# The last stage of a four-stage transformer kernel: chunks of 512 tokens, a wider window for its scatters, and results of a token side by side

## What is computed

```
xn = (x1 - mean(x1)) * rsqrt(var(x1) + 1e-5) * ln_gamma + ln_beta
abel_out = gelu(xn @ abel_w + abel_b)
logits = xn @ moe_gate_w + moe_gate_b            # 8 experts
topw, topi = top_k(logits, 2);  topw = softmax(topw)
h  = gelu(xn @ ew1[e] + eb1[e])                  # 128 -> 256, for the two experts of a token
eo = h @ ew2[e] + eb2[e]                         # 256 -> 128
moe_out = sum of the two eo, weighted by topw
moe_out = moe_out @ expm(gens[0]) @ expm(gens[1]) @ expm(gens[2])
gate = sigmoid(concat(abel_out, moe_out) @ gc_w + gc_b)     # one number per token
result = x + x1 + abel_out * (1 - gate) + moe_out * gate
```

## Time and profile before

| | us |
|---|---|
| time, median of 3 runs (1953.77 to 1956.29) | 1954.69 |
| the profiled execution, its own time | 1961.08 |
| its span, first to last instruction | 1959.3 |
| PE busy over the span | 1404.7 |
| DVE busy | 1144.8 |
| ACT busy | 684.6 |
| POOL busy | 658.8 |

### The profile page before, as it was taken

One profiled execution on the slowest core, in us unless ns is written; L12 is line 12 of the kernel. 1 busy time (PEld: TensorE's weight loads), 2 busy tenths in 40 slices (PEclk: granted clock), 3 DMA queues, 4 the chain that ended last, 5 costly groups with the idle time before them and its releaser, 6 DMA issues.

```text
span 1959.3 us, 36114 instructions
## 1 busy us (share of the span) xinstructions
PE 1404.7 (72%) x13280; PEld 931.6 (48%) x13280; DVE 1144.8 (58%) x3564; ACT 684.6 (35%) x1106; POOL 658.8 (34%) x903
## 2 busy tenths in 40 slices
PE   4587878788887888786347994777777956737750
PEld 2344434343434444343335663666666846636640
DVE  4576667768686767663543552666766653224437
ACT  1144444444444444444102341232333311124532
POOL 2022232323132222221141003566666725534442
PEclk9599999999999999998558996677767655557885
DMA  3646355452727253540611110111111120112224
GB/s 94 99 70 94 49 76 87 70 93 32 121 34 117 37 89 62 89 71 10 220 31 37 37 37 19 49 49 35 36 35 32 30 75 32 40 59 64 67 60 114
DMA packets 88673, 125.06 MB, mean 64 GB/s; under 512 B 17376, under 2 KB 62949, under 8 KB 87604
## 3 DMA queue, kind: packets, MB, share of 16 engines
q1 hardware_dynamic: 80004, 108.90, 29.2%
q0 software_dynamic: 7392, 13.39, 2.2%
q10 hardware_dynamic: 1104, 0.48, 0.1%
HBM read 30.15 MB, written 19.34 MB: 25 GB/s over the span
## 4 chain that ended last, share of the span: by engine, by line
PE 37%; DVE 28%; issue 8%; DMA 8%; POOL 8%; ACT 5%; SPq 4%; DVEq 0%; ACTq 0%; POOLq 0%
PE S L392 5%; DVE first L588 5%; PE A L421 4%; PE S L871 4%; SPq L330 3%; PE S L384 3%; PE S L403 3%; DMA yq<-yq,id 3%; DVE S L593 3%; POOL xq L1874 2%; DVE sc L1373 2%; DVE mx L1372 2%; DMA Kp<-rck 2%; PE A L1229 2%; PE S L166 2%
## 5 line engine op out<-in xcount | busy, mean ns | idle before, releaser
L495 ACT ACTIVATE P<-S 128x1024 f32<-128x1024 f32 (+3 forms) x384 | 310.1, 809 | 402.2 <-PE S L403 398.7
L662 POOL TENSOR_SCALAR_AFFINE_SELECT P<-P 128x256 f32<-128x256 f32 (+1 forms) x256 | 114.8, 450 | 546.1 <-ACT P L495 546.0
L392 PE MATMUL S<-Kp,Qp 120*128 120x512 f32 (+3 forms) x768 | 240.9, 399 | 77.1 <-DMA Kp<-rck 48.3
L403 PE MATMUL S<-Qp,Kp 121*128 121x512 f32 (+3 forms) x768 | 238.2, 394 | 71.7 <-DVE first L588 25.8
L593 DVE CUSTOM_DVE_ANT_0 S<-S,later 128x512 f32<-128x512 f32 (+3 forms) x512 | 239.8, 515 | 64.8 <-PE S L392 64.0
L392 PEld LDWEIGHTS S<-Kp,Qp 120*128 120x128 f32 x768 | 130.6, 201 | 217.3 <-issue 89.7
L588 DVE TENSOR_REDUCE first<-S 128x2 f32<-128x1024 f32 x128 | 156.6, 1224 | 117.0 <-PE S L392 116.5
L403 PEld LDWEIGHTS S<-Qp,Kp 121*128 121x128 f32 x768 | 133.8, 198 | 151.1 <-DVE first L588 46.0
L421 PE MATMUL A<-P,V 128*9 128x512 f32 (+3 forms) x1536 | 180.0, 516 | 3.7 <-POOL P L662 3.7
L1304 ACT ACTIVATE pr<-sc 128x1024 f32<-128x1024 f32 x32 | 34.3, 1072 | 208.6 <-DVE sc L1373 208.6
L1879 POOL DMA_INDIRECT yq<-yq,id x71 | 72.7, 1024 | 89.7 <-DVE yq L1825 74.6
(11 more groups left out here) (311 smaller groups left out, 2747.5 us busy)
## 6 DMA issues: line engine op xcount, KB each, us to landing
Qp<-rcq SPq DMA_DIRECT2D x64, 256.0 KB
Kp<-rck SPq DMA_DIRECT2D x64, 256.0 KB
Qp<-rcq SPq DMA_DIRECT2D x64, 128.0 KB
Kp<-rck SPq DMA_DIRECT2D x64, 128.0 KB
xq<-xq SPq DMA_DIRECT2D x71, 72.0 KB, 1.9
Qp<-cq SPq DMA_DIRECT2D x64, 64.0 KB
Kp<-ck SPq DMA_DIRECT2D x64, 64.0 KB
w<-in_w SPq DMA_DIRECT2D x4, 1024.0 KB, 12.2
```

Source lines behind the costliest of these rows:

```text
L392: ins = te.matmul(S[s][:, 512 * h:512 * h + n], Q[0:120, h, 128 * qt:128 * qt + 128], K[0:120, h, 512 * part:512 * part + n], start=True, ...
L403: ins = te.matmul(S[s][:, 512 * h + c:512 * h + 512], K[0:121, h, 128 * kb:128 * kb + 128], Q[0:121, h, 512 * qh + c:512 * qh + 512], star ...
L495: se.activation(k.P[(w.n - 1) % NP0][:, :, c:512], S[s][:].rearrange("p (j k) -> p j k", j=2)[:, :, c:512], ACT.Exp, scale=SCALE0).then_in ...
L662: ge.affine_select(P[:, :, start:c + 128], P[:, :, start:c + 128], [[0, 2], [1, wide]], ALU.is_ge, 0.0, base=start - c, channel_multiplier ...
```

## The change

It has six parts, all in the last stage.

1. Chunks in routing are 512 tokens (`G` = 4 blocks, `NC1` = 8 chunks) in place of 1024. Numbers, transposed blocks and positions (`n2`, `nT`, `posu`) get three buffers for two.
2. The list: all of `normal(1)` but its last item comes before `top` of chunk 0; from then on the items of `normal(c + 1)` and `route(c)` alternate, and `ab` stands behind `rank`. `fold` has four parts, after chunks 1 to 4.
3. `id` gets eight buffers and the results five (`NY1`). `id` of tile t waits for the scatter of tile t - 8, and the result of tile t for that of t - 5.
4. The gate's product of a result comes from the second matmul: `Rg` is R with one more column, R times the gate's weights, and `fold` makes weights and bias of 129 columns (`er`). The four products per chunk in the mixing (L1848) go.
5. Rows of `yq` are 132 wide, the product in column 128.
6. `idt` gives both results of a token adjacent rows, and the rows of a partition's four tokens follow each other, so one DMA per chunk in the mixing takes 4224 bytes per partition in one piece.

```diff
-CAP, RW = B * T + 128, 144
+CAP, RW, YW = B * T + 128, 144, 132
 NE1 = 2 * NT + 7
-NX1 = 6
+NX1, NY1 = 6, 5
+G, NC1 = 4, 8
...
-        self.n2 = [two(f"n2{q}", [128, 8, RW]) for q in range(2)]
-        self.nT = two("nT", [128, 1024])
+        self.n2 = [two(f"n2{q}", [128, G, RW]) for q in range(3)]
+        self.nT = [sb(f"nT{q}", [128, 128 * G]) for q in range(3)]
...
-        self.id = [sb(f"id{i}", [128, 1], U32) for i in range(4)]
-        self.yo = [sb(f"yq{i}", [128, 128]) for i in range(4)]
+        self.id = [sb(f"id{i}", [128, 1], U32) for i in range(8)]
+        self.yo = [sb(f"yq{i}", [128, YW]) for i in range(NY1)]
...
         def route(c):
             self.slot["lg1", c] = o.add("lg1", c, ring="A").slot
-            o.add("ab", c, ring="S")
-            yield
             yield
             o.add("top", c)
             yield
             self.slot["rank", c] = o.add("rank", c, ring="A").slot
+            o.add("ab", c, ring="S")
             yield
             o.add("pos", c)
             yield
 
         all_of(normal(0))
-        for c in range(B):
-            run_beside(normal(c + 1) if c + 1 < B else (), route(c), 0, 1.0)
-            if c < 3:
-                o.add("fold", c, ring="S")
+        run_beside(normal(1), route(0), 4, 1.0)
+        for c in range(1, NC1):
+            run_beside(normal(c + 1) if c + 1 < NC1 else (), route(c), 1, 1.0)
+            if c < 5:
+                o.add("fold", c - 1, ring="S")
...
-            for h in range(2):
-                ye.dma_start(k.y[u % 3][h][:], y_v[h, :, 4 * u:4 * u + 4, :]).then_inc(p.sem(f"d_yb{u % 3}").h, 16)
+            ye.dma_start(k.y[u % 3][:].rearrange("p i h d -> p (i h d)"), y_v[u]).then_inc(p.sem(f"d_yb{u % 3}").h, 16)
...
+                    ve.tensor_copy(k.Rg[:, 0:128], p.R[:])
+                    ve.tensor_tensor_reduce(k.junk[:], p.R[:], sm["gcb"][:], 1.0, 0.0, ALU.mult, ALU.add, k.Rg[:, 128:129]).then_inc(p.sem("v_Rg").h, 1)
...
-            if t > 3:
-                dve.wait_ge(p.sem(f"d_yq{t % 4}"), 16 * (t // 4))
-            ve.tensor_copy(k.id[t % 4][:], k.xg[t % NX1][:, 128:129]).then_inc(p.sem("v_id").h, 1)
+            if t > 7:
+                dve.wait_ge(p.sem(f"d_yq{(t - 8) % NY1}"), 16 * ((t - 8) // NY1 + 1))
+            ve.tensor_copy(k.id[t % 8][:], k.xg[t % NX1][:, 128:129]).then_inc(p.sem("v_id").h, 1)
         elif w.kind == "down1":
             t = w.at[0]
             dve.wait_ge(p.made("down1"), w.n)
-            ve.tensor_tensor(k.yo[t % 4][:], A[s][:, 0:128], k.b2R[:, bass.ds(expert[t] * 128, 128)], ALU.add).then_inc(p.done("down1").h, 1)
+            if t >= NY1:
+                dve.wait_ge(p.sem(f"d_yq{t % NY1}"), 16 * (t // NY1))
+            ve.tensor_tensor(k.yo[t % NY1][:, 0:129], A[s][:, 0:129], k.er[:, bass.ds(expert[t] * 129 + 16 * 129, 129)], ALU.add).then_inc(p.done("down1").h, 1)
...
-            for i in range(4):
-                dve.then(ve.tensor_tensor_reduce(k.junk[:], mo[:, i, :], sm["gcb"][:], 1.0, 0.0, ALU.mult, ALU.add, sM[:, i:i + 1]))
-            ve.tensor_tensor(sM[:], sM[:], k.sA[:, 4 * u:4 * u + 4], ALU.add).then_inc(p.sem("v_sum").h, 1)
+            ve.tensor_tensor(sM[:], mo[:, :, 128], k.sA[:, 4 * u:4 * u + 4], ALU.add).then_inc(p.sem("v_sum").h, 1)
```

More of the change, by code:

```diff
@@ L1568, in ffn1_sync @@
     sp.wait_ge(p.sem("d_pad"), 16 * 9)
-    for q in range(2):
-        sp.wait_ge(p.sem(f"d_xq{q}"), 16 * 16 * B // 2)
+    for q in range(3):
+        sp.wait_ge(p.sem(f"d_xq{q}"), 16 * 2 * G * len(range(q, NC1, 3)))
     sp.wait_ge(p.sem("v_row"), 1)
@@ L1577, in ffn1_sync @@
         ye.dma_start(k.xg[t % NX1][:], k.xq[bass.ds(row, 128), :]).then_inc(p.sem(f"d_xh{t % NX1}").h, 16)
-    for i in range(4):
-        sp.wait_ge(p.sem(f"d_yq{i}"), 16 * len(range(i, NE1, 4)))
+    for i in range(NY1):
+        sp.wait_ge(p.sem(f"d_yq{i}"), 16 * len(range(i, NE1, NY1)))
     o_v = p.out.rearrange("(n p) d -> p n d", p=128)
-    y_v = k.yq.rearrange("(h n p) d -> h p n d", h=2, p=128)
+    y_v = k.yq.rearrange("(u p r) d -> u p (r d)", u=8, p=128)
     for u in range(8 + 2):
@@ L1601, in ffn1_tensor @@
             pe.wait_ge(p.sem("v_n2"), c + 1)
-            turn_over(te, p, S[s], k.n2[c % 2][0][:, :, 0:128], 8).then_inc(p.made("nT").h, 1)
+            turn_over(te, p, S[s], k.n2[c % 3][0][:, :, 0:128], G).then_inc(p.made("nT").h, 1)
         elif w.kind == "lg1":
-            q = w.at[0] % 2
+            q = w.at[0] % 3
             pe.wait_ge(p.done("nT"), w.n)
-            for i in range(8):
+            for i in range(G):
                 ins = te.matmul(A[s][:, 8 * i:8 * i + 8], k.nT[q][:, 128 * i:128 * i + 128], k.small["mw"][:], start=True, stop=True)
@@ L1618, in ffn1_tensor @@
             oh = k.oh[:].rearrange("p n e -> p (n e)")
[L1619 to L1623, removed]
+            te.matmul(A[s][:, 0:8 * G], k.small["tri"][:], oh, start=True, stop=False)
+            for d in range(1, G):
+                te.matmul(A[s][:, 8 * d:8 * G], k.small["one"][:], oh[:, 0:8 * (G - d)], start=False, stop=(d == G - 1))
+            for i in range(G):
+                ins = te.matmul(A[s][:, 64:72], k.small["one"][:], oh[:, 8 * i:8 * i + 8], start=(i == 0), stop=(i == G - 1))
             ins.then_inc(p.made("rank").h, 1)
@@ L1627, in ffn1_tensor @@
             pe.wait_ge(p.sem("d_f1e"), 16 * 3)
-            for i in range(8):
-                e, j = 4 * f + i // 2, i % 2
-                lhsT = k.b2s[:, i, :] if f == 2 else k.e2T[:, e, 128 * j:128 * j + 128]
-                ins = te.matmul(S[s][:, 128 * i:128 * i + 128], lhsT, p.R[:], start=True, stop=True)
+            pe.wait_ge(p.sem("v_Rg"), 1)
+            for i in range(6):
+                b, at = 6 * f + i, 512 * (i // 3) + 129 * (i % 3)
+                lhsT = k.e2T[:, b // 2, 128 * (b % 2):128 * (b % 2) + 128] if b < 16 else k.b2s[:, b - 16, :]
+                ins = te.matmul(S[s][:, at:at + 129], lhsT, k.Rg[:], start=True, stop=True)
             ins.then_inc(p.made("fold").h, 1)
@@ L1745, in ffn1_vector @@
             ve.memset(t[:, :, 128:RW], 0.0)
+    for t in k.yo:
+        ve.memset(t[:, 129:YW], 0.0)
     for w in k.items:
@@ L1918, in program @@
         p.again(f"d_xh{i}", f"d_xg{i}", 16 * len(range(i, NE, NX)))
-    for i in range(4):
-        p.again(f"d_yq{i}", f"d_yg{4 + i}", 16 * NT // 8)
-    for i in range(2):
-        p.again(f"d_xq{i}", f"d_yg{2 + i}", 16 * NT // 8)
+    for i in range(NY1):
+        p.again(f"d_yq{i}", f"d_yg{i}", 16 * NT // 8)
+    for i in range(3):
+        p.again(f"d_xq{i}", f"d_yg{NY1 + i}", 16 * NT // 8)
     for i in range(3):
```

95 lines of the change are left out of this document (47 added, 48 removed).

## The result

The changed kernel took 1924.32 us (median of 4 runs, 1919.55 to 1925.85), the kernel before 1955.49 (4 runs, 1953.77 to 1960.64) on the same chip: ratio 0.9833, 95% interval 0.9809 to 0.9858, so 31 us faster, where 1922 had been forecast. The profiled execution has a span of 1922.0 for 1959.3. A later pair gave 0.9855 (0.9816 to 0.9893), but a third one, on another chip, only 0.9944 (0.9911 to 0.9978). The experiments show which part of the gain is missing there. One execution of experiment 4 took 2975 us, and the ratio leaves it out.

What follows compares the result with a forecast made beforehand. Scatter was taken as bound by POOL's DMAs and gaps, the loop by `id` waiting for landings, mixing by DVE and loads. Terms +12 - 37 - 8 = -33 gave 1928 profiled, 1922 median; range 1904 to 1946 for 8 in 10.

Steps and rivals of the forecast that it cites:

- Gaps: Scatter, between POOL's groups of DMAs: six gaps of 9.9 us and a seventh of 5.5, for 16, 16 and 8.
- the five steps: One scatter gap: `rs` 1.5 us, scaling 1.05, top-2 and one-hot 2.3, rank on PE 3.6, positions 1.5.
- A chunk ahead: Scatter: preparing the next chunk's norm a chunk ahead doesn't take the norm out of a gap; seven gaps replace three.
- Scatter +12: Scatter of 64 indirect DMAs to `xq`: ends at 1754.0 against 1742.4, 12 us lost.
- Loop -37: Loop over 71 tiles: eight tiles in 13.0 us for 17.4, the limit passing to the engines; 37 us gained.
- Mixing -8: Mixing of eight chunks: 4.6 us each for 5.49, limited by landing, issue and ScalarE's scaling; 8 us gained.
- The sum: Whole kernel: +12 - 37 - 8 = -33, profiled execution 1928, median 1922.
- The rounds don't shrink: Rival, scatter: gaps as long for 512 tokens as for 1024, seven losing 49 to 51 us; 1960; 5%.
- the window doesn't open: Rival, tile loop: landings grow beyond 8 us with the number under way, eight tiles stay at 17; 1959; 3%.
- POOL's DMAs lengthen: Rival, tile loop: each DMA costs 0.3 us more beside a busier DVE, 20 us gained there; 1939; 10%.
- TensorE at full clock in the rounds: Rival, scatter: six ranks lose 1.7 us each, in all -43; 1912; 13%.
- TensorE at the lower clock in the loop: Rival, tile loop: PE takes 1.92 us per tile, 11 us gained there, 7 in all; 1948; 12%.

Runs made afterwards that it cites:

- experiment 4: Changed kernel with chunks of 1024 tokens and the old order of norms and products again: 1955.30 (ratio 0.9912) and, run again, 1955.37 (0.9921) to the kernel before.
- experiment 6: Changed kernel with DVE's routing ahead of the next chunk's third norm and POOL's DMAs behind both `rs`: 1912.21, ratio 0.9790 to the kernel before.
- experiment 7: Changed kernel with DVE's block `pre` split into six items, one a tile: 1914.34, ratio 0.9804 to the kernel before.
- experiment 2: Kernel before with eight `id` buffers and three result buffers, nothing else changed: 1951.99, ratio 0.9919 to the kernel before.
- experiment 8: Changed kernel with the output's store one turn later on the SP queue: 1921.09, ratio 0.9826 to the kernel before.
- third group: Kernels run together on one chip; the changed kernel without an edit took 1963.06 there against 1970.41 for the kernel before, ratio 0.9944.
- kernels 1 to 4: Kernel before with five, then three result buffers and eight `id`: 0.9935, 0.9919; changed kernel with DVE's gate products, then 1024-token chunks: 1.0007, 0.9912.
- first group: Four kernels with parts of the change, run together on one chip, where the kernel before took 1971.63.
- second group: Kernels run together on one chip; the changed kernel without an edit took 1925.42 there against 1957.75 for the kernel before, ratio 0.9855.

## Why the prediction was right

- **Gaps** (forecast 9.9 and 5.5): 9.77 and 5.39, each of the five steps within 0.1 us. The halving held for what is passes or rows, and the fixed waits were kept. "A chunk ahead" took nothing out of a gap, as forecast, and experiment 6 shows how much was left in that order.
- **Scatter +12**: +10.4, and +9.9 against experiment 4. From the tables' load to the end the forecast had 165.0, the trace 163.8: 1.1 less to the first DMA (0.6 of it the load itself), 0.9 less in the gaps, 0.8 more in the DMAs.
- **Loop -37**: -35.6; eight tiles 13.29 for 13.0, and no wait of `id`. The stall behind `pre`, 1.1 to 1.9 us on PE, was the larger part of what kept it from 10.9: experiment 7 takes 1.3 us away and leaves 1.0. That five result buffers are needed was an assumption of the forecast that experiment 2 does not bear out.
- **Mixing -8**: -8.0. The limit was the landing behind the store, as named; experiment 8 shows it by moving the store.
- **The sum.** The parts add up to -33.3 for -33, closer than any of them, because the misses of scatter and loop have opposite signs; that is luck. The medians differ by 31.2. The profiled execution was to take 1928 and took 1923.7; 4.0 of these 4.3 us are the earlier tables' load.
- **The rivals.** "The rounds don't shrink" and "the window doesn't open" fell with the gap of 9.8 and the 35.6 us. "POOL's DMAs lengthen" fell too: `yq`'s 71 DMAs are 1005 ns each, 980 in most rows. By the rule of the Trainium skill ("SBUF — State Buffer", "SBUF: two separate sides") a DMA of POOL stands until a copy of DVE in a two-port mode ends. In the trace hardly anything of that shows at the weight copies: the DMAs that start with or within one take 0.98 to 1.04. The wide sums of `pre` are what holds DMAs: seven start 0.17 to 0.53 us into such a sum, end 0.86 to 0.88 us after it, and take 1.02 to 1.40. About one in eight, they do not set the loop's time, and the kernel before had eight such DMAs of 1.28 to 1.41. "TensorE at full clock in the rounds": 0.54.
- **"TensorE at the lower clock in the loop"** (12%, 1948, a gain of 7 us) is the one that the first pair alone would have buried. On the third group's chip, and by kernels 1 to 4 on the first group's, it came half true: the clock was 0.85 to 0.91 and not 0.50, and late starts, which the forecast did not have, did the rest. That 7 us were gained in the third group, as this rival says, is luck: its step is half of what happened. The forecast was right where the loop is fast; the third group's 1963 lies outside its range of 1904 to 1946.

## What to carry to other kernels

Price a chain of hand-overs step by step from one round's timeline, split each step into what scales with the size and what doesn't, and count how often the round now comes: here smaller chunks cost ten microseconds inside a change that gained thirty. Where a window of buffers is too small, find the wait that stands in front of other engines' work (`id`, a small copy) before adding large buffers. When a loop passes from a DMA's latency to the engines, short stalls of TensorE begin to count, and a vector block of 3 us in the loop is best dealt out over the iterations.

## What the runs showed of the hardware

- The same program differs by more from chip to chip than from run to run. The kernel before took 1955, 1958, 1970 and 1972 us on four occasions; the changed kernel 1924, 1925 and 1963, where its runs on the last chip span 17. From the second group's chip to the third's, the kernel before lost 13 us and the changed one 38. Between the profiled executions of the changed kernel it is 47.4: 18.9 before the tables' load, in stages that no kernel here changes, 0.8 in the scatter and 27.8 in the loop. The kernel before seems to lose nearly all of its 13 in those earlier stages. Its last stage there can be estimated from each of the eight traces of the first and third group: the last stage of that kernel plus what its median gained. Seven of the estimates are 368 to 373 us and one is 380, and the kernel's own trace, of the first pair, has 370.3. That before's waits for landings cover the slower hand-overs would explain it, but no trace of the kernel before was taken on the slower chips, so this is argued and not shown. Compare only kernels that ran on the same chip, and repeat the unchanged kernel there.
- After PE had stood 1.5 to 2 us its granted clock sometimes stayed at 1.00 and sometimes fell to 0.50, for 3.4 us in one chip's trace and 6.8 in another's. With the stalls taken out it stayed at 1.00 over 93 us (experiment 7).
- An indirect DMA of POOL that starts 0.1 to 0.5 us into a sum of 128x512 on DVE ends 0.85 to 0.88 us after that sum, and takes up to 1.41 us where most take 0.98 (the traces of both kernels).
- A load of 528 KB in rows of 4.2 KB per partition landed in 3.9 us (median of eight), no later than one of two loads of 256 KB in pieces of 512 B (4.14); the median of the sixteen smaller ones is 3.5.
